# Value products of the last three attention tasks issued in two parts of the queries

## The reference

```
x = L0_attn_x                                   # (1, 2048, 128)
q, k, v = x @ W_qkv.T                           # 16 heads of 8, rope on q and k
scores = q @ k.T / sqrt(8), causal
attn = softmax(scores) @ v
x = layernorm(x + attn @ W_o.T)
w = quantised to 4 bits (ffn_kernel)
x = layernorm(x + (x @ w + bias + (x @ a) @ b))
```

## Time and profile before

| | us |
|---|---|
| median of 3 runs | 507.91 |
| lowest, highest | 506.31, 509.31 |
| profiled execution | 506.48 |
| its span, first to last instruction | 504.8 |
| TensorE busy | 454.8 (90%) |
| VectorE busy | 383.8 (76%) |
| ScalarE busy | 313.8 (62%) |
| GpSimd busy | 86.7 (17%) |
| mean granted TensorE clock | 0.96 |

### The profile page before, as it was taken

The page is one execution under the profiler, slowest core; times in us unless marked ns, Lnnn a source line. Parts: engine busy times, 40 slices in busy tenths (PEclk is TensorE's granted clock), DMA queues, the critical chain, the costliest instruction groups (busy, mean ns, idle before and its releaser), DMA issues.

```text
span 504.8 us, 7980 instructions
## 1 busy us (share of the span) xinstructions
PE 454.8 (90%) x3007; PEld 201.1 (40%) x3007; DVE 383.8 (76%) x494; ACT 313.8 (62%) x629; POOL 86.7 (17%) x137
## 2 busy tenths in 40 slices
PE   5888989299899999999999999999999999999942
PEld 2444434043333444434444454334343433434421
DVE  1776799478989999998999999999899560413563
ACT  2233664077257678847677686787767888788500
POOL 8344302000100010010021321001002002232342
PEclk9998999689979999999999999999999999999985
DMA  8322211110000001110000011100000000000001
GB/s 242 123 86 83 86 44 54 52 55 9 1 1 2 2 24 54 54 45 5 1 1 1 8 53 53 53 13 1 2 1 3 0 3 3 1 23 1 21 0 43
DMA packets 11046, 16.51 MB, mean 33 GB/s; under 512 B 849, under 2 KB 6241, under 8 KB 11009
## 3 DMA queue, kind: packets, MB, share of 16 engines
q1 hardware_dynamic: 11008, 16.01, 9.0%
HBM read 10.37 MB, written 5.24 MB: 31 GB/s over the span
## 4 chain that ended last, share of the span: by engine, by line
PE 71%; DVE 10%; issue 5%; ACT 3%; DMA 2%; POOL 2%; POOLq 0%; DVEq 0%; SPq 0%; ACTq 0%
PE sT L1019 25%; PE oP L1035 24%; PE ring L979 13%; DVE pmax L814 9%; ACT probs L745 3%; PE ring L990 2%; DMA qS<-mrows 2%; PE ring L1044 1%; PE sT L948 1%; PE ring L986 1%; POOL rstd L656 1%; PE ring L998 1%; PE sT L963 0%; PE ring L1060 0%; PE sT L953 0%
## 5 line engine op out<-in xcount | busy, mean ns | idle before, releaser
L745 ACT ACTIVATE probs<-sT 128x512 f32<-128x512 f32 (+2 forms) x576 | 289.0, 578 | 121.9 <-PE sT L1019 120.8
L814 DVE TENSOR_REDUCE pmax<-ring 128x2 f32<-128x1024 f32 (+2 forms) x272 | 318.5, 1220 | 43.8 <-PE ring L979 24.2
L1019 PE MATMUL sT<-qS,kS 64*128 64x512 f32 (+3 forms) x640 | 178.1, 427 | 10.7 <-DMA qS<-mrows 8.3
L979 PE MATMUL ring<-kS,qS 64*128 64x512 f32 (+3 forms) x640 | 142.9, 424 | 6.7 <-DVE pmax L814 3.7
L1035 PE MATMUL oP<-probs,vP 128*9 128x512 f32 (+3 forms) x1280 | 144.8, 533 | 2.4 <-POOL probs L681 2.4
L1019 PEld LDWEIGHTS sT<-qS,kS 64*128 64x128 f32 x640 | 87.7, 186 | 121.2 <-ACT probs L745 93.7
L681 POOL TENSOR_SCALAR_AFFINE_SELECT probs<-probs 128x512 f32<-128x512 f32 x64 | 40.5, 636 | 334.0 <-ACT probs L745 333.9
L979 PEld LDWEIGHTS ring<-kS,qS 64*128 64x128 f32 x640 | 65.4, 187 | 60.1 <-DVE pmax L814 34.5
L1035 PEld LDWEIGHTS oP<-probs,vP 128*9 128x9 f32 x1280 | 20.5, 88 | 43.3 <-issue 24.9
L854 DVE RECIPROCAL rsum<-ring 128x16 f32<-128x16 f32 x16 | 4.0, 251 | 25.7 <-PE ring L1044 25.7
L990 PE MATMUL ring<-causal,ident_h 128*128 128x256 bf16 x96 | 18.8, 278 | 0.0
(11 more groups left out here) (117 smaller groups left out, 192.8 us busy)
## 6 DMA issues: line engine op xcount, KB each, us to landing
qS<-q_parts SPq DMA_DIRECT2D x52, 64.0 KB
kS<-k_parts SPq DMA_DIRECT2D x52, 64.0 KB
cs<-rope_tables_dram SPq DMA_DIRECT2D x4, 512.0 KB, 7.3
q_parts<-qp SPq DMA_DIRECT2D x4, 512.0 KB, 2.8
k_parts<-kp SPq DMA_DIRECT2D x4, 512.0 KB, 2.9
x_sb<-in_L_attn_x_dram SPq DMA_DIRECT2D x4, 256.0 KB, 6.4
qS<-mrows SPq DMA_DIRECT2D x32, 8.0 KB
out_dram<-rot SPq DMA_DIRECT2D x2, 256.0 KB, 2.3
```

Of the source, the lines that this page charges most:

```text
L745: nc.scalar.activation(probs[:, J % PRING, heads[0]:heads[-1] + 1:2, lo:CH], sT[:, at % SBANKS, 0:len(heads) * (CH - lo)].rearrange("p (h ...
L814: nc.vector.tensor_reduce(dst, src, AX.X, ALU.max).then_inc(unit_free, 1)
L979: last = nc.tensor.matmul(ring[:, slot_of(e), hl, at:at + w], qS[rows, b, c, hp, ii * TOK:(ii + 1) * TOK], kS[rows, b, kk, hp, 0:w], start ...
L1019: last = nc.tensor.matmul(sT[:, at % SBANKS, x * w:(x + 1) * w], kS[rows, b, j // TPC, hp, (j % TPC) * TOK:(j % TPC + 1) * TOK], qS[rows, ...
```

## The change

In tasks 13, 14 and 15 a value product whose step has more than 256 queries left is issued as two events: the queries up to 256, and those from 256 to 512. With 512 queries these are two parts of 256, with 384 (the second diagonal step) parts of 128 and 256. Steps with 256 or 128 queries stay whole. Of the 24 steps of the three tasks 18 are cut (9 + 1 in task 13, 5 + 1 in task 14, 1 + 1 in task 15). The columns are the same, the matmuls 72 more. Events are now (n, j, x) with x as the part. The second part alone counts up probs_free, and only the first of the first step starts the accumulation in oP. The search prices the parts by their width, with 2 x 0.06 us for each, and is free to lay other events between them.

```
+HALVED_FROM = 13
+
+def value_parts(n, j):
+    lo = first_query(TASKS[n][1], j)
+    return [(lo, CH)] if n < HALVED_FROM or CH - lo <= CH // 2 else [(lo, CH // 2), (CH // 2, CH)]
...
-    V = [(n, j) for n, (g, c) in enumerate(TASKS) for j in range(steps(c))]
+    V = [(n, j, x) for n, (g, c) in enumerate(TASKS) for j in range(steps(c)) for x in range(len(value_parts(n, j)))]
...
         elif kind == "PV":
-            n, j = e
+            n, j, x = e
             c = TASKS[n][1]
             self.v += 1
-            self.values = self.values[1:]
-            end = self.whole(2 * self.SWITCH + 0.853 * (CH - first_query(c, j)) / CH, ready)
-            i = self.probs.index(FAR)
-            self.probs = self.probs[:i] + (end + 0.15,) + self.probs[i + 1:]
-            if j == steps(c) - 1:
+            lo, hi = value_parts(n, j)[x]
+            last = hi == CH
+            end = self.whole(2 * self.SWITCH + 0.853 * (hi - lo) / CH, ready)
+            if last:
+                self.values = self.values[1:]
+                i = self.probs.index(FAR)
+                self.probs = self.probs[:i] + (end + 0.15,) + self.probs[i + 1:]
+            if last and j == steps(c) - 1:
...
-            def values(n, j):
+            def values(n, j, x):
                 (g, c), J = TASKS[n], STEP[(n, j)]
-                lo = first_query(c, j)
-                if j == 0:
+                lo, hi = value_parts(n, j)[x]
+                if j == 0 and x == 0:
...
                 for h in range(HG):
-                    last = nc.tensor.matmul(oP[VW * h:VW * h + VC, lo:CH], vP[:, j, HG * g + h, :], probs[:, J % PRING, h, lo:CH],
-                                            start=j == 0, stop=j == TASK_END[n])
-                last.then_inc(probs_free, 1)
+                    last = nc.tensor.matmul(oP[VW * h:VW * h + VC, lo:hi], vP[:, j, HG * g + h, :], probs[:, J % PRING, h, lo:hi],
+                                            start=j == 0 and x == 0, stop=j == TASK_END[n])
+                if hi == CH:
+                    last.then_inc(probs_free, 1)
```

More of the change, by code:

```diff
@@ L175, in choices @@
         if self.values:
-            n, j = self.V[self.v]
+            n, j, x = self.V[self.v]
             ready = max(self.values[0], self.clear if j == 0 else 0.0)
-            out.append((max(self.pe, ready), ready, "PV", n, j))
+            out.append((max(self.pe, ready), ready, "PV", n, j, x))
         for ready, *e in self.due:
@@ L283 @@
 Course.S_PE = acc(Course.S, lambda x: pair_cost([CH - first_query(TASKS[x[0]][1], x[1])] * len(score_sets(TASKS[x[0]][1], x[1])[x[2]])))
-Course.V_PE = acc(Course.V, lambda x: 2 * Course.SWITCH + 0.853 * (CH - first_query(TASKS[x[0]][1], x[1])) / CH)
+Course.V_PE = acc(Course.V, lambda x: 2 * Course.SWITCH + 0.853 * (value_parts(x[0], x[1])[x[2]][1] - value_parts(x[0], x[1])[x[2]][0]) / CH)
 Course.S_ACT = acc(Course.S, lambda x: 0.09 + len(score_sets(TASKS[x[0]][1], x[1])[x[2]]) * (CH - first_query(TASKS[x[0]][1], x[1])) / 1200)
@@ L323, in schedule @@
         out.append(event)
-        if event == ("PV", 1, 0):
+        if event == ("PV", 1, 0, 0):
             out.append(("W",))
@@ L342 @@
 SET = {e[1:]: i for i, e in enumerate(e for e in SCHEDULE if e[0] == "S")}
-PV_AT = {e[1:3]: i for i, e in enumerate(e for e in SCHEDULE if e[0] == "PV")}
+PV_AT = {e[1:3]: i for i, e in enumerate(e for e in SCHEDULE if e[0] == "PV" and e[3] == 0)}
 DIAGONAL = {e[1:3]: i for i, e in enumerate(e for e in SCHEDULE if e[0] == "S" and e[3] == 0 and e[2] >= steps(TASKS[e[1]][1]) - TPC)}
@@ L769, in _ @@
                     exponentials(*e[1:])
-                if e[0] == "PV" and e[2] == TASK_END[e[1]]:
+                if e[0] == "PV" and e[2] == TASK_END[e[1]] and e[3] == 0:
                     flush_o(e[1])
```

## The result

The changed kernel takes 508.59 us in the median of 20 runs (506.51 to 510.11), the kernel before 507.44 in 20 runs taken beside them (505.36 to 509.59). The ratio is 1.0027, with a 95% interval of 1.0014 to 1.0039, which is 1.4 us slower, 0.7 to 2.0 (the medians differ by 1.15). This is inside the range and within the half per cent called no change, but it is clear of noise, and the forecast of 0.14 us faster had the wrong sign.

The account below looks back on a forecast made before the run. TensorE and ScalarE, handing three PSUM banks back and forth, were taken as the bound, then a tail of small steps. Terms 0.4 + 1.06 + 0.25 - 1.85 = -0.14 us gave 507.8 us, range 505.0 to 510.6.

Parts of the forecast that it names:

- First part: Run-up to POST(2,5), tasks 13 and 14: split products and lone scores make it +0.4 us later, bounds -1.0 and +2.0.
- stretch A: End of O(12) to end of task 13 step 7's value product: 18.70 us before, forecast 19.66, growing 0.96.
- rival 2: Waits in stretch A and task 14 stay, bound to ScalarE freeing banks: +2.2, so 510.0 us; chance 0.16.
- Second part: POST(2,5) to O(14): task 14 step 5's mask now behind GpSimd's root, TensorE waits 1.0; +1.06 us.
- Third part: O(14) to POST(1,3): the score set ahead waits for its bank, then a half product; +0.25 us.
- Fourth part: From POST(1,3) to the end: earlier O(15) and POST(0,2) copy let POST(0,3)'s VectorE work start at 11.4; -1.85 us.
- Rival 1: Splits are free, a half 0.49 and a lone score 0.22: POST(2,5) at -1.5, median 505.9 us; chance 0.22.
- Rival 3: New VectorE order at the end brings nothing, O(15) late or POST(1,5) binding: 1.85 lost, 509.6 us; chance 0.10.
- The rule weighed: TensorE: rows' 0.12 us fixed per value-product run, fitting drains on tiling change, against the skill's nearly free cuts.

Follow-up runs that it names:

- parts_apart: Kernel before, products cut in task 13 only, a score set moved between the parts in seven of its first eight steps; 509.25 us, ratio 1.0020.
- masks_first: Changed kernel with GpSimd's root of POST(2,5) behind the masks of steps 5 to 7 of task 14, NORM(2,1) later; 507.13 us, ratio 0.9992.
- all_three: Kernel before, uncut, with reordered steps behind the last value product, unused matmuls in the tail's gaps, and masks ahead of POST(2,5)'s root; 504.93 us, ratio 0.9965.
- clock_kept: Changed kernel with unused matmuls on TensorE in the waits for the mask of step 3 of task 15 and ahead of O(15); 507.14 us, ratio 0.9994.
- cut_in_place: Kernel before, its order kept, the 18 value products cut into two parts side by side with nothing between; 506.98 us, ratio 0.9991.
- all_three_clock_450: Kernel before with all_three's edits, plus five short unused matmuls between score sets of steps 8 to 10 of task 13; 503.87 us, ratio 0.9910.

## Why the prediction was wrong

**What bounds the kernel** was read rightly: two engines that hand three banks to each other, and behind them a chain of small steps. Between these two profiles nothing outside the four terms came up; the fall of the clock near 450, in other profiles, did.

**First part (+0.4 forecast, +0.96 measured).** The step that failed is the sum for the new stretch A, 19.66, with the words "I find next to no waits left". The prices held: 0.55 for a half, 0.42 for a lone set. But 20.07 us were measured, so A grew by 1.37 and not by 0.96: three pairs of score sets still waited for banks (429.63, 436.76, 446.89), 0.16, 0.20 and 0.26 us, while the other nine pairs were 0.03 cheaper each and the POST units 0.11 dearer together. That rival 2's mechanism could be true in part was in the text, and it got too little weight in the first term. The shrinking behind A came as forecast: 0.83 us of the growth were gone at O(13), where 0.66 to 0.96 had been given. I also took the waits of before as something that could be filled. parts_apart shows what filling them in this way costs: each change to and fro is 0.36 us of an engine that had 1.42 of slack in 18.70. Task 14 came as its own sum had it (0.6 + 0.6 - 0.8 = 0.4, measured +0.42), but the term for both, 0.4, was the low end of the prediction's own parts: 0 to 0.3 at O(13) and 0.4 behind it.

**Second part (+1.06, +1.06).** The walk was right at the points that count (5.17 and 7.14), and the size with it. Its heading, a mask moved behind the root, was not the cause: the wait grew only from 0.61 to 0.67 us, and the rest is 1.00 us more of other work on TensorE between POST(2, 5) and O(14). masks_first and all_three show that 1.14 us remain between the two orders when no mask stands behind that root. Only the three masks together were moved; the one of step 5 by itself was not tried. Of the detail, TensorE reached the step at 4.5 us and not at 4.1, so that the wait was 0.67 and not 1.0; what came behind did not depend on it.

**Third part (+0.25, +0.21).** The size was right; no run tests the reason given for it.

**Fourth part (-1.85, -0.88).** The order on VectorE does what was worked out: 27.04 us with the clock kept, 2.11 below before. The step that failed is "POST(1,5) at about 8.4, its VectorE work 1.16 later": the walk put TensorE's groups in at full clock. The group came at 8.88 and its VectorE work 1.75 later, at 10.63, and everything behind it on VectorE moved with it, from the 11.4 of the walk to 12.42. With the clock kept (clock_kept) the three times are 8.26, 9.43 and 11.22. The two sentences beside it held in what they conclude: the matmuls of POST(0, 3) ran later than given, to 11.5, but were still over ahead of VectorE, and the chain behind is as long as before (15.85 and 15.90). The walk itself left TensorE 0.87 us of standing still ahead of O(15), behind a wait for the mask. Before, 1.43 us of waiting in that place left the clock up, so the earlier trace rows did not forbid full clock; but the clock falls in this tail in the trace of before too, at 487.8, and the walk has no word on it. clock_kept gives the price: 1.23 us.

With the first term at +0.96 and the fourth at -0.88 the sum is +1.35 and not -0.14. Rival 1 (free splits) is out by the 0.55 and 0.43 rows and parts_apart. Rival 2 is partly right: score sets still waited for banks in stretch A, its own sign, for 0.62 us. Rival 3, which would have the end's gain lost because O(15) is late, named another mechanism than the one that took half of it.

**The rule weighed.** cut_in_place and parts_apart bear on both sentences of the Trainium skill. Two adjoining parts take 0.98 us, as a whole product does. The Trainium skill, "TensorE: Matmul & The Clock Gate", section "Back-to-back issue gap", puts 2.5 ns beside the columns, for an isolated matmul; for the four matmuls that a cut adds this is an estimate of 0.01 us at most, and the trace agrees to that. What costs is the change between scores and value products: 0.12 us at the product and about 0.2 at a lone score set. The Trainium skill, "TensorEngine Tiling (Array Packing)", section "Key Properties", says that a change of the tiling mode drains TensorE; the rows fit that, but no run here tells a drain from another price of the change.

**What is open.** How often the clock falls near 450 in the order of before. If it did in half of the executions, the mean of before would hold 0.8 us of it, and the changed kernel, with no fall in its four profiles, should be only some 0.6 us behind and not the 1.4 (0.7 to 2.0) that was timed. The profiles are too few to say. Nor did the runs divide the 0.96 us up to POST(2, 5) between the cut and the order found for it. And the timed ratios of all_three and all_three_clock_450 are not what their profiles would have.

## What to carry to other kernels

Before cutting work finer so that two engines mesh better, price the change between kinds of work on the engine that has the least slack, not the cut: here the cut was free and each alternation cost 0.36 us. When a shared list orders several engines, read the order of each of them; the gain of this change came from one copy on VectorE that nobody had meant to move, and a wait for a mask on GpSimd of 0.6 us, the same in both kernels, was worth 0.9 us to mend. A wait that stands out in the new trace is the cause of a difference only if the old trace lacks it. And in a tail of short steps, carry TensorE's granted clock through the walk, as a wait ahead of a chain can slow what stands behind it, here by 1.23 us: unused matmuls in the gaps of the tail, with the better order of the last steps, made a kernel at 0.9926 (0.9896 to 0.9955) of before.

## What the runs showed of the hardware

- A score set of 512 queries alone between two value products takes 0.43 us of TensorE (441.02 to 441.45), two take 0.43 as well, three 0.65. Cutting a value product in two costs nothing where the parts adjoin (0.98 us both ways).
- After waits of 1.90 and 0.80 us with a product of 0.41 us between them the clock fell to 1.2 GHz, from about 483.6 to 487.0. After waits of 1.43 and 0.28 us before, it stayed at 2.4 GHz. In three of six executions of one order it fell behind a stretch in which TensorE was shown busy for 1.55 of 2 us, in the other three it did not, with the same 1.55. Equal order gave equal times to 0.04 us wherever the clock was the same.
- Four normalising instructions of VectorE (L895 before, L908 after, 128x128 each) took 1.75 us together beside two masks on GpSimd, 1.42 beside one, 2.08 beside three, and 1.11 alone.
